# One attention and mixture-of-experts layer on one core: the opening in another order, packs by whole batches, z before x

## The reference, cut to what matters

```python
x  = L0_attn_x                      # 4 x 256 x 512, float32
xn = layernorm(x)
# attention, 32 heads of 16, 8 groups of keys and values, causal
q, (k, v) = xn @ Wq, xn @ Wkv       # reshaped to heads and groups
ctx = softmax(mask(q k^T) / 4) v
attn = ctx @ Wo + bo
# experts: 16, each token takes the best 4, hidden 256; one shared expert for all
scores = sigmoid(xn @ gate_w.T) + bias
cw = normalised scores of the top 4
ffn = sum_e cw[:, e] * (silu(xn @ Wg[e].T) * (xn @ Wu[e].T)) @ Wd[e].T
ffn += (silu(xn @ Sg.T) * (xn @ Su.T)) @ Sd.T
out = x + attn + ffn
```

## Time and profile before

| | us |
|---|---|
| median of 3 runs | 569.83 (568.35 to 570.0) |
| the profiled execution | 569.64 |
| its span in the profile | 567.9 |
| TensorE busy | 468.4 |
| VectorE busy | 365.0 |
| GpSimd busy | 268.3 |
| ScalarE busy | 263.5 |
| mean granted TensorE clock | 0.943 |

### The profile page before, as it was taken

One profiled execution on the slowest core, in us unless ns is written; L12 is line 12 of the kernel. 1 busy time (PEld: TensorE's weight loads), 2 busy tenths in 40 slices (PEclk: granted clock), 3 DMA queues, 4 the chain that ended last, 5 costly groups with the idle time before them and its releaser, 6 DMA issues.

```text
span 567.9 us, 9993 instructions
## 1 busy us (share of the span) xinstructions
PE 468.4 (82%) x2968; PEld 344.9 (61%) x2968; DVE 365.0 (64%) x606; ACT 263.5 (46%) x386; POOL 268.3 (47%) x234
## 2 busy tenths in 40 slices
PE   0995789968989997789878878997978899889880
PEld 0964578846667775367656655765656557667650
DVE  7377874676567957375779871787775546766510
ACT  2531212216555655165668642655736335645610
POOL 2002593304764652267546863573757336364510
PEclk9997999987998998899999899998989999889976
DMA  7804963336666557465687883668655534334222
GB/s 285 329 28 111 226 231 100 107 118 214 158 130 152 113 104 212 142 157 96 141 236 190 277 162 60 154 139 205 175 104 107 95 56 83 68 54 81 38 38 37
DMA packets 32060, 78.23 MB, mean 138 GB/s; under 512 B 4288, under 2 KB 11200, under 8 KB 28800
## 3 DMA queue, kind: packets, MB, share of 16 engines
q0 software_dynamic: 11936, 27.53, 26.8%
q1 hardware_dynamic: 17808, 43.96, 23.5%
q10 hardware_dynamic: 2256, 6.03, 5.0%
HBM read 54.04 MB, written 23.33 MB: 136 GB/s over the span
## 4 chain that ended last, share of the span: by engine, by line
PE 45%; DVE 15%; issue 8%; DMA 8%; ACT 8%; ACTq 6%; POOL 5%; SPq 2%; DVEq 1%; POOLq 1%
PE psum L1093 24%; PE psum L1221 5%; DMA q_parts<-stage 3%; ACT wsplit L573 3%; DVE negm L906 3%; PE psum L1187 2%; PE psum L1203 2%; POOL xn L446 2%; PE psum L1058 2%; ACTq L266 2%; PE psum L1115 2%; PE psum L1042 2%; POOL out L457 1%; PE psum L1103 1%; ACTq L264 1%
## 5 line engine op out<-in xcount | busy, mean ns | idle before, releaser
L1093 PE MATMUL psum<-wsplit,xgT 128*128 (+1 forms) x660 | 175.0, 416 | 0.2
L1093 PEld LDWEIGHTS psum<-wsplit,xgT 128*128 128x128 f32 x660 | 125.8, 197 | 30.3 <-issue 2.7
L457 POOL DMA_INDIRECT out<-ysb,tab x48 | 88.6, 1845 | 105.1 <-ACT ysb L606 84.2
L1093 PE MATMUL psum<-wsplit,zT 128*128 (+1 forms) x336 | 95.3, 420 | 29.0 <-DVE zT L898 29.0
L1093 PEld LDWEIGHTS psum<-wsplit,zT 128*128 128x128 f32 x336 | 61.6, 193 | 48.9 <-issue 37.6
L948 DVE TENSOR_TENSOR xgT<-psum,xgT 128x512 fp32r<-128x512 f32 x47 | 32.3, 688 | 65.4 <-ACT xgT L569 65.3
L437 POOL DMA_INDIRECT xg<-xn_rows,tab x47 | 51.9, 1104 | 29.6 <-PE psum L1231 20.0
L648 ACT ACTIVATE xn<-psum 128x1536 f32<-128x1536 f32 x32 | 46.5, 1453 | 40.6 <-PE psum L1189 40.6
L975 DVE TENSOR_TENSOR plo<-xn,phi 128x1536 f16<-128x1536 f32 x32 | 63.5, 1984 | 1.0
L446 POOL TENSOR_SCALAR_AFFINE_SELECT xn<-xn 128x512 f32<-128x512 f32 x64 | 55.3, 1060 | 7.9 <-ACT xn L648 7.8
L462 POOL TENSOR_TENSOR wsplit<-wraw,wsplit (+1 forms) x16 | 39.1, 2446 | 41.1 <-ACT wsplit L573 41.1
(11 more groups left out here) (180 smaller groups left out, 655.9 us busy)
## 6 DMA issues: line engine op xcount, KB each, us to landing
wraw<-wexp SPq DMA_DIRECT2D x17, 1024.0 KB, 6.1
wraw<-wexp SPq DMA_DIRECT2D x17, 512.0 KB, 4.6
q_parts<-stage SPq DMA_DIRECT2D x16, 192.0 KB
q_pack<-q_parts ACTq DMA_DIRECT2D x6, 384.0 KB, 4.6
xn<-x SPq DMA_DIRECT2D x4, 512.0 KB, 5.2
xn_rows<-xn SPq DMA_DIRECT2D x8, 256.0 KB, 7.6
ctxs<-x SPq DMA_DIRECT2D x8, 256.0 KB, 3.2
out<-ysb SPq DMA_DIRECT2D x8, 256.0 KB, 3.2
```

The source lines that it names most:

```text
L457: nc.gpsimd.indirect_dma_start(out=out, out_offset=rows_of(s), in_=ysb[:, par, :], in_offset=None, compute_op=ALU.add).then_inc(y_out[par] ...
L1093: last = MM(dst, lhs(a, k), split_weights(place, w, c), start=m == 0, stop=m == len(products) - 1)
```

## The change

1. **Order on TensorE in the opening.** Unit 3 is projected behind the ranks instead of before them. For each tile the order is now: transpose of z of n-1, gate/up of n, unit 4+n, maxima (at n = 2, 3, 4, 5 instead of 1, 3, 5, 7), table (n = 4 and 6 instead of 3 and 5), down of n-1. Unit 4 uses bank 0. The first transposed maxima are made at n = 6, and the first slot's rows are transposed before the last down.
2. **Order on VectorE and ScalarE.** They follow it. `columns` is one per tile over n = 0 to 3; `slot_tokens`, `slot_experts`, `slot_gates` are at n = 5, 6, 7. `gated(0)` stands within the slot arithmetic. The one-hot sums are four scalar_tensor_tensor of 128 elements instead of products of 512. The first expert's weights are split within n = 5 to 7. The shared expert's split weights are in place 1 instead of 0.
3. **Values.** Their three parts are made by ScalarE (`value_part`, n = 2, 4, 6) and GpSimd (`value_rest`), no longer by VectorE.
4. **Packs.** k in DRAM has the rows outermost, and its units are stored in two DMAs each with runs of half the length. There are two buffers of packs (`q_packs`, `k_packs`; the second lies in `xT` and `wqk_sb`). Batch 0 is packed as before; batch 1 by SyncE before it announces the experts' weights; batches 2 and 3 by ScalarE, one whole-batch DMA behind each of the first six slots.
5. **Slots.** z goes to bank 3 instead of the bank of the down product, and the transposed maxima to `PV` instead of bank 3. z is transposed and split before x. The wait for the eviction of y (`y_sb`) stands before the down product instead of before z's transpose. The branch holds only the weights' halves, and the number is loaded ahead; the place is computed from it.

```diff
-            for u in range(EARLY):
+            for u in range(EARLY - 1):
...
             last.then_inc(ranks_ps, 1)
+            project(EARLY - 1)
...
             for n in range(NT):
-                if EARLY + n < UNITS:
-                    pe.wait_ge(rem_done, EARLY + n)
-                    project(EARLY + n)
                 if n:
                     z_transpose(n - 1, (n - 1) % 2, XT)
                 pe.wait_ge(xs_low, n + 1)
-                gate_up(n % 2, 0)
-                if n % 2:
-                    if n == 1:
-                        pe.wait_ge(packed[0], HALF_PACK)
+                gate_up(n % 2, SHARED)
+                if EARLY + n < UNITS:
+                    pe.wait_ge(rem_done, 1 if n == 0 else EARLY + n - (n == 1))
+                    project(EARLY + n)
+                if n in MAXIMA_AT:
+                    if MAXIMA_AT[n] == 0:
+                        pe.wait_ge(packed[0], PACK)
...
@@ VectorE, opening
             for n in range(NT):
+                if n:
+                    z_low(n - 1, (n - 1) % 2, XT)
+                    gated(n, n % 2)
+                if n + 2 < NT:
+                    xs_low_part(n + 2)
+                if n < 4:
+                    columns(n)
                 if EARLY + n < UNITS:
                     remainder(EARLY + n)
-                if n:
-                    z_low(n - 1, (n - 1) % 2, XT)
-                gated(n, n % 2)
-                if n + 2 < NT:
-                    xs_low_part(n + 2)
+                if n in MAXIMA_AT:
+                    maxima(MAXIMA_AT[n], MAXIMA_AT[n])
                 if n:
                     shared_out(n - 1)
...
@@ VectorE, one-hot sums
+            def of_choice(out_, values):
+                for k in range(TOPK):
+                    own.did(V.scalar_tensor_tensor(out=out_[:, :, k, :], in0=rt[:, 12, :, :], scalar=float(k + 1), in1=values,
+                                                   op0=ALU.is_equal, op1=ALU.mult))
+                own.wait()
...
@@ SyncE
+            for i in range(2):
+                sp.wait_ge(parts_out[i], units_out(UNITS - 2 + i))
+            sp.wait_ge(proj_ps, UNITS)
+            sp.wait_ge(xs_low, NT)
+            for i in range(6):
+                pack_one(sp, i, 1)
             sp.wait_ge(table_ps, 2)
...
@@ GpSimd, opening
+            def value_rest(c):
+                pool.wait_ge(v_high, c + 1)
+                pool.wait_ge(v_rest, c)
+                nc.gpsimd.tensor_tensor(val, val, val_part[c], ALU.subtract).then_inc(v_rest, 1)
             for u in range(EARLY + 3, UNITS):
                 third_part(u)
+                if u < UNITS - 1:
+                    value_rest(u - EARLY - 3)
...
@@ ScalarE, batches
                     numerators(b, g)
-                    if g % 4 == 3 and not last:
-                        pack_half(act, g // 4, b + 1)
                     for j in BESIDE[g]:
-                        slot_parts(s, 1 - j % 2, not (last and j + 1 >= SPS - 1))
+                        here, number = ahead
+                        z_high(s + (U1 - 1), 1 - par)
+                        if s + 1 < NSLOT:
+                            x_high(s + 1, 1 - par)
+                            gate_up_high(number)
...
                         y_evac(b, j)
+                        if 0 < b < B - 1 and j < 6:
+                            pack_one(act, j, b + 1)
...
@@ TensorE, batches
+                        z_transpose(s + (U1 - 1), 1 - j % 2)
                         if not (last and j + 1 >= SPS - 1):
                             rows_transpose(s + 1, 1 - j % 2, 8 * SPS * b + 16 * ((j + 1) // 2 + 1))
-                        pe.wait_ge(y_sb, s + 1)
-                        z_transpose(s + (U1 - 1), 1 - j % 2)
                         if j == BESIDE[g][-1] and (g == 3 or g == 7 and not last):
+                            pe.wait_ge(csum_done, G * b + g + 1)
                             maxima_transpose(G * b + (g + 5), 1 - g // 4)
...
+                            if g == 4:
+                                pe.wait_ge(packed_next, PACK * (b + 1))
                             scores_for_max(b, G * b + (g + 4), (g + 4) % G)
                         pe.wait_ge(w_low[1], prev[1])
+                        pe.wait_ge(y_sb, s + 1)
                         down(s + (U1 - 1), 1 - j % 2, prev[0])
```

More of the change, by code:

```diff
@@ L63 @@
 EARLY = 4
+MAXIMA_AT = {2: 0, 3: 1, 4: 2, 5: 3}
+SHARED = 1
 SCALE = HD ** -0.5
@@ L484, in sequence @@
                             gather(SPS * b + (j + 3), 1 - j % 2, SPS * b + (j + 2))
-                        if not (last and j == SPS - 1):
-                            down_low_of(SPS * b + j)
+                        s = SPS * b + j
+                        if 0 < s < NSLOT:
+                            down_low_of(first_in(s))
                         add_rows(b, j)
                 add_attention(b)
+            pool.wait_ge(proj_ps, UNITS)
+            pool.wait_ge(lo_done, UNITS)
+            nc.gpsimd.memset(k_packs[1][QROWS:P], 1.0).then_inc(ones_next, 1)
             gather(0, 0, None)
@@ L739, in _, with gated @@
             ws_low_part(0)
+            def gated(n, par):
+                dve.wait_ge(th_done, n + 1 - (n >= U1) if isinstance(n, int) else n)
+                if not isinstance(n, int) or n:
+                    dve.wait_ge(z_done, n)
+                own.did(V.scalar_tensor_tensor(out=zh[:, :], in0=th[:, par, :], scalar=1.0, in1=bank(GU, FI),
+                                               op0=ALU.add, op1=ALU.mult))
+                own.wait()
+                if not isinstance(n, int) or n >= 2:
+                    dve.wait_ge(zt_ps, n - 1)
+                V.scalar_tensor_tensor(out=zz[:, par, :], in0=zh[:, :], scalar=0.5, in1=psum[:, GU, FI:2 * FI],
+                                       op0=ALU.mult, op1=ALU.mult).then_inc(z_done, 1)
             def over_experts(a):
@@ L997, in attention_out, with sequence @@
                     V.tensor_tensor(att[:, qt, :], bank(WO[qt]), bo_sb[:, :], ALU.add).then_inc(att_sb, 1)
-            def sequence(b, last):
+            def sequence(b, last, number):
                 for g in range(G):
@@ L1002, in sequence @@
                         s = SPS * b + j
-                        slot_parts(s, 1 - j % 2, not (last and j + 1 >= SPS - 1))
-                        if not (last and j == SPS - 1):
+                        z_low(s + (U1 - 1), 1 - j % 2)
+                        if s + 1 < NSLOT:
+                            x_low(s + 1, 1 - j % 2)
+                            gate_up_low(number)
+                        if s < NSLOT:
                             gated(s + U1, j % 2)
+                        number = first_in(s + 2) if s + 2 < NSLOT else None
                         if j == BESIDE[g][0] and not (last and g >= 4):
@@ L1277, in sequence @@
                         elif g == G - 1:
+                            if not last:
+                                pe.wait_ge(nmT_sb, 2 * b + 3)
                             weighted(b, g)
```

317 lines of the change are left out of this document (149 added, 168 removed).

## The result

The changed kernel takes 561.07 us (median of 4 runs, 556.69 to 562.46), the one before 569.09 beside it (4 runs, 567.75 to 570.0). The ratio is 0.988, 95% interval 0.9836 to 0.9923. That is a gain, but a quarter of the forecast one, and 561 lies outside the range of 516 to 556. The profiled execution of the changed kernel took 562.46 us, with a span of 560.7, against 569.64 and 567.9.

A forecast was written before the change was run, and what follows sets the result against it. TensorE, busy 468.4 of 567.9 us, was taken as the bound, with its idle time and low clock to gain from. 569.6 - 11 (opening) - 24 (batches) = 534.6, so 535 us; likely 526 to 545, outer range 516 to 556.

The forecast's parts named there:

- (1): Opening: unit 3 projected behind the ranks, so the first gate/up product starts at about 43 us, not 54.34.
- (4): Opening, tiles 0 to 2: the unit between gate/up and z covers the ScalarE and VectorE round that stood bare before.
- (5): Opening: the stall for unit 4's store stays; it lands at about 73 and TensorE stops about 2.6 us.
- (7): End of opening: work moved ahead of the last two tiles; stops of 3.05, 2.38, 2.00 us become about 1 or less.
- two value subtractions on GpSimd: Opening: taking turns on the port pair could cost VectorE up to their whole length, 5 us less gain.
- (a): Batches: packs cut from 36 issues on ScalarE to 12, batch 1's on SyncE; 10.1 us of stalls go.
- (b): Batches: z in bank 3, transposed first, wait for y's eviction behind gate/up; 8.0 us go, nothing comes back.
- Rival D: Stalls removed are replaced one for one, another input of the same product being as late: 570 us, chance 0.04.
- (c): Batches: other waits for z, 11.2 us, shrink as z goes ahead of x on ScalarE and VectorE; 4 us gained.
- (d): Batches: new wait of the maxima for the last pack of batches 2 and 3, about 1 us, twice: +2.
- (e): Batches: fewer idle gaps raise TensorE's granted clock; 4 us back, bounds 0 and 9.
- (f): Batches: exchanging the banks of z and the transposed maxima adds waits only on things finished slots before: 0.

The follow-up runs named there:

- the fastest: Changed kernel with transposed maxima in bank 2, down-weight subtraction on VectorE, batch 1's packs issued by ScalarE one per slot; whole computation: 0.9639 to the kernel before, 547.05 us.

## Why the prediction was wrong

**The opening, -11, came to -7.8.** (1) was right to a microsecond (42.04 for 43). (4): in the first tile, the unit covered the round but for 1.76 us before the transpose at 50.36. (5): the store was to land at about 73 and landed at 74.35, and the stall stops TensorE for 4.91 us, not 2.6. (7) failed: the three stops at the end, to be "about 1 us each or less", were 2.60, 2.28 and 2.86 us. I had moved the slot's experts and the weights' halves forward on VectorE without asking what they now stand in front of. The 5 us that the prediction named for the two value subtractions on GpSimd did not show: beside them the longest stretch of a VectorE operation was 0.6 us (1.32 instead of 0.69 us at 99.69), and the rest had an input in PSUM. And I had misread: no L829 ran alone, all four had more than 1 us of GpSimd's column products beside them; those of 1.21 us had started ahead of GpSimd's operation.

**The batches, -24, came to +0.5.** (a) was right, where the packs are only left out. (b) failed as a mechanism: the wait removed was not the last one, the product behind it needed z's low half as late as before. "nothing comes back" was wrong, 7.1 of 8.0 us came back in the next two waits. Rival D's mechanism held here. (c) makes up for it in part: with z split first (b) and (c) give half of their sum, and with the packs out all three give -21.7, the forecast sum. (d) was +2; the late packs cost 4.7, of which the wait that (d) priced is 1.2 us, once. (e) can't be seen in the granted clock, 0.943 and 0.946. TensorE is busy 8.3 us less over the four batches, for the same products, but idle some 9 us more. (f), priced at 0, costs between nothing and 7 us.

Two steps that had no term made the rest. **Batch 1's packs on SyncE** stood in (a) as "issued by SyncE before the batches", at no cost: I counted issue time, which SyncE has, and not the 1.9 MB that they put, beside Wo's 1 MB, ahead of expert 2's weights. That is 7 us of the first batch. **GpSimd's subtraction** of the down weights had no term: I weighed the taking of turns for the opening's value subtractions alone. In the batches it costs 16.3 us instead of 8.3. TensorE's waits suggest why, what it holds up is now nearer to TensorE's path, but neither the way nor the size of the difference (3 to 13 us) is shown. Together 15 us; with the late packs' 2.7 above forecast, (e)'s 4 and the opening's 3 this makes 25 of the 27 us by which the forecast missed. That is a sum of single differences with intervals of some 4 us each, and these need not add: the edits put together gave less than their sum. That it comes so close is in part luck.

**What stays open.** The second batch takes 105 to 115 us in all versions, 109.0 in the fastest; VectorE is busy 80.4 of 112 there in the changed kernel, and no run took that load away as a whole. Which edit of the change moved the maxima's split and the weights' halves beside GpSimd's subtraction is not settled either, nor how much of that subtraction's cost runs through VectorE and how much through GpSimd's own list.

## What to carry to other kernels

A wait that is taken from one engine's list is worth only what the next input of the same work comes earlier: before booking it, look up when that input is ready, and on which in-order list it stands. Bulk transfers cost twice: by their issue, where they stand in bursts in a busy engine's list (11.7 us for six bursts here), and by what urgent load comes behind them (7.4 us here); spread them one per step. An elementwise operation on GpSimd may hold up a far smaller one on VectorE with two SBUF inputs for its whole length, so after a reordering ask anew which small operations lie beside it.

## What the runs showed of the hardware

VectorE's subtraction over 128x32 in SBUF takes 198 ns on the mean without GpSimd's large one and 2.25 us beside it, eleven times as long. Not every operation is held up: five of the contexts' sums (`csum`, a reduction with its input in PSUM) ran beside it and took 0.51 us as the others do, and z's low half, with one input in PSUM, keeps its length (409 to 427 ns in all 56, five of them beside it). An operation with its inputs in SBUF that started ahead of GpSimd's kept its length too (L829 of the kernel before, 1.21 us; 1.84 where GpSimd's was first). A load of weights, whose median from issue to landing is 4.4 us in the changed kernel, took 18.17 us behind 3 MB of other transfers from the same queue (6.9 us behind 1 MB in the kernel before), and moving those behind the next load moved the delay to a gather of rows on another queue (5.4 us).
